# Four neighbouring tokens to a partition in a three-layer macaron kernel

## The reference, cut to what matters

```python
def _apply_rope(x, sin, cos):
    x1 = x[..., ::2]
    x2 = x[..., 1::2]
    r = jnp.stack([x1 * cos - x2 * sin, x1 * sin + x2 * cos], axis=-1)
    return r.reshape(x.shape)

q = (src @ Wq)...; k = (src @ Wk_c @ Wk)...; v = (src @ Wv_c @ Wv)...
sin, cos = _rope_sincos(Tt, DH)
q = _apply_rope(q, sin, cos)
k = _apply_rope(k, sin, cos)
attn = softmax(einsum('bhqd,bhkd->bhqk', q, k) / sqrt(DH))
x = _rmsnorm(src + (attn @ v) @ Wo, norm1_w)
# then an MLP and eight gated experts on x, token by token, and a second norm
```

## Time and profile before

| | |
|---|---|
| median of the runs | 834.25 us |
| the profiled execution | 834.06 us, of which its span is 832.0 us |
| TensorE busy | 804.7 us (97%) |
| VectorE busy | 664.6 us (80%) |
| ScalarE busy | 501.9 us (60%) |
| GpSimd busy | 353.5 us (42%) |
| mean granted TensorE clock | 0.997 |
| moved by DMA | 37.83 MB in 24700 packets |

### The profile page before, as it was taken

One profiled execution on the slowest core, in us unless ns is written; L12 is line 12 of the kernel. 1 busy time (PEld: TensorE's weight loads), 2 busy tenths in 40 slices (PEclk: granted clock), 3 DMA queues, 4 the chain that ended last, 5 costly groups with the idle time before them and its releaser, 6 DMA issues. The chain is left out here.

```text
span 832.0 us, 13459 instructions
## 1 busy us (share of the span) xinstructions
PE 804.7 (97%) x4436; PEld 308.7 (37%) x4438; DVE 664.6 (80%) x1303; ACT 501.9 (60%) x1073; POOL 353.5 (42%) x760
## 2 busy tenths in 40 slices
PE   8899999999999999999999999999999999999996
PEld 3323334334333343332323232233433434355453
DVE  6999987697789758887989999988988687673355
ACT  3267664475467627765877777777764475376441
POOL 2564328615331353424442357334253623442534
PEclk9999999999999999999999999999999999999999
DMA  4565203010200010020010323204102200000000
GB/s 119 129 168 128 81 2 78 19 58 11 70 2 2 20 62 2 9 74 3 3 51 32 78 81 83 76 14 107 37 21 58 77 2 14 1 15 2 1 13 14
DMA packets 24700, 37.83 MB, mean 45 GB/s; under 512 B 6464, under 2 KB 22080, under 8 KB 23048
## 3 DMA queue, kind: packets, MB, share of 16 engines
q1 hardware_dynamic: 24149, 36.25, 15.5%
q10 hardware_dynamic: 483, 0.74, 0.3%
HBM read 27.03 MB, written 9.11 MB: 43 GB/s over the span
## 5 line engine op out<-in xcount | busy, mean ns | idle before, releaser
L1387 ACT ACTIVATE probs<-ps 128x512 f32<-128x512 f32 x768 | 414.4, 598 | 228.0 <-PE ps L957 205.1
L1178 DVE TENSOR_REDUCE maxes<-ps 128x1 f32<-128x512 f32 x768 | 479.1, 681 | 47.6 <-PE ps L924 45.5
L924 PE MATMUL ps<-k_aug,q_aug 72*128 72x512 bf16 (+1 forms) x768 | 246.2, 382 | 3.5 <-ACT k_aug L1358 0.7
L957 PE MATMUL ps<-q_aug,k_aug 75*128 75x512 bf16 (+1 forms) x704 | 231.8, 383 | 3.3 <-DMA q_aug<-maxT 1.3
L984 PE MATMUL ps_out<-probs,v_aug 128*18 128x512 f32 x1408 | 185.4, 598 | 1.7 <-ACT probs L1387 1.0
L924 PEld LDWEIGHTS ps<-k_aug,q_aug 72*128 72x128 bf16 (+1 forms) x768 | 64.3, 96 | 162.8 <-issue 107.1
L1058 PE MATMUL ps<-w,hidden 128*128 128x512 f32 x256 | 118.7, 596 | 0.0
L957 PEld LDWEIGHTS ps<-q_aug,k_aug 75*128 75x128 bf16 (+1 forms) x704 | 59.0, 97 | 136.3 <-issue 88.9
L1279 DVE TENSOR_TENSOR prod<-ps,gate 128x512 f32<-128x512 f32 x56 | 38.7, 691 | 54.5 <-PE ps L1058 43.6
L1579 POOL TENSOR_TENSOR prod<-prod 128x512 f32<-128x512 f32 x28 | 35.5, 1268 | 85.2 <-DVE prod L1279 68.8
L1499 POOL TENSOR_SCALAR max_parts<-maxes 128x16 bf16<-128x16 f32 (+1 forms) x38 | 10.9, 288 | 141.6 <-DVE maxes L1178 141.4
(11 more groups left out here) (157 smaller groups left out, 755.3 us busy)
## 6 DMA issues: line engine op xcount, KB each, us to landing
q_aug<-qk_parts SPq DMA_DIRECT2D x7, 1152.0 KB
k_aug<-qk_parts SPq DMA_DIRECT2D x21, 384.0 KB
qk_parts<-parts SPq DMA_DIRECT2D x48, 128.0 KB, 2.3
q_aug<-qk_parts SPq DMA_DIRECT2D x11, 288.0 KB
k_aug<-qk_parts SPq DMA_DIRECT2D x27, 96.0 KB
qk_parts<-parts SPq DMA_DIRECT2D x24, 64.0 KB, 2.0
X<-in_x_dram SPq DMA_DIRECT2D x4, 256.0 KB, 4.6
w<-in_ffn_W_experts_dram SPq DMA_DIRECT2D x2, 512.0 KB, 5.8
```

Source lines behind the costliest of these rows:

```text
L924: pe.matmul(bank(use[i]), q_aug[p0:p1, r, at, qt * 128:(qt + 1) * 128], k_aug[p0:p1, r, at, :], start=True, stop=True).then_inc(bank_full[ ...
L957: pe.matmul(bank(use[i]), k_aug[p0:p1, r, at, kt * 128:(kt + 1) * 128], q_aug[p0:p1, r, at, :], start=True, stop=True).then_inc(bank_full[ ...
L1178: dve.tensor_reduce(maxes[:, u % 2, qt, at:at + 1], full(use[0]), AX.X, ALU.max).then_inc(bank_free[use[0][0]], 1)
L1387: act.activation(probs[:, step % P_RING, c:c + exp_run(u), :], both(use), ACT.Exp, scale=scale)\
```

## The change

A partition now holds four neighbouring tokens: token 4p + t lies in tile t of partition p. A load or store of a whole sequence moves 2048 contiguous bytes a partition where it moved four pieces of 512 bytes. The store of a single tile takes every fourth row of the output. Along the row of `xT`, column 128t + p is now token 4p + t, so every use of the tables reads them in that order: four runs of 128 elements, and within a run every fourth element (16 bytes apart). The other operand and the result are seen with the same shape, and are read and written contiguously. The tables themselves are loaded as before.

```diff
+        def by_tiles(a):
+
+            return a.rearrange("d (t p) -> d t p", p=128)
+
+        def table(a):
+            return a[:, :].rearrange("d (p t) -> d t p", p=128)
+
         def rotate(eng, seq, own_wait, u, qk):
 
             c, s, q = rotated(u, qk)
-            seq(eng.tensor_tensor(s, s, sinT[:, :], ALU.mult))
+            seq(eng.tensor_tensor(by_tiles(s), by_tiles(s), table(sinT), ALU.mult))
...
-            sp.dma_start(X[:, 0, :, :], x[0].rearrange("(t p) c -> p t c", p=128)).then_inc(x0_loaded, 16)
+            sp.dma_start(X[:, 0, :, :], x[0].rearrange("(p t) c -> p t c", p=128)).then_inc(x0_loaded, 16)
...
-                sp.dma_start(X[:, b, :, :], x[b].rearrange("(t p) c -> p t c", p=128)).then_inc(x_loaded, 16)
+                sp.dma_start(X[:, b, :, :], x[b].rearrange("(p t) c -> p t c", p=128)).then_inc(x_loaded, 16)
...
-                    sp.dma_start(out[b].rearrange("(t p) c -> p t c", p=128), X[:, b, :, :]).then_inc(stored, 16)
+                    sp.dma_start(out[b].rearrange("(p t) c -> p t c", p=128), X[:, b, :, :]).then_inc(stored, 16)
...
-                    sp.dma_start(out[batch(u), t * 128:(t + 1) * 128, :], X[:, batch(u), t, :]).then_inc(stored, 16)
+                    sp.dma_start(out[batch(u)].rearrange("(p t) c -> p t c", p=128)[:, t, :], X[:, batch(u), t, :]).then_inc(stored, 16)
...
-                    ins = dve.tensor_tensor(c, o, cosT[:, :], ALU.mult)
+                    ins = dve.tensor_tensor(by_tiles(c), by_tiles(o), table(cosT), ALU.mult)
...
-                        dve.tensor_tensor(s, full(use[1]), sinT[:, :], ALU.mult).then_inc(bank_free[use[1][0]], 1)
+                        dve.tensor_tensor(by_tiles(s), by_tiles(full(use[1])), table(sinT), ALU.mult).then_inc(bank_free[use[1][0]], 1)
```

## The result

| | before | after |
|---|---|---|
| median of 19 runs each | 835.39 us | 837.46 us |
| lowest run | 833.78 us | 837.03 us |
| profiled execution, span | 834.06, 832.0 us | 837.46, 835.5 us |
| TensorE, VectorE, POOL busy | 804.7, 664.6, 353.5 us | 807.0, 671.8, 358.4 us |

The ratio after to before is 1.0027, with a 95% interval of 1.0015 to 1.0039: slower beyond its interval, and within the 0.5% that the prediction calls "same". The traces and the lowest runs lie 3.3 to 3.5 us apart, the medians only 2.1 us. The kernel before came out at 835.39 us in these 19 runs, 1.1 us above the three runs on which the forecast stood.

The account below looks back on a forecast made before the run. VectorE bounds 21 to 48 us, both engines are nearly full 48 to 128 and 384 to 576, TensorE bounds 576 to 800. Terms -0.1 + 0 + 0.56 + 0.3 + 0.6 + 0.3 = +1.7 on 834.06 give 835.7 us, range 833.0 to 839.2.

Parts of the forecast that it names:

- x: What a stepped table read adds to one VectorE multiplication: taken as 0.2 us, range 0 to 0.52.
- Load, -0.1 us: First load of X, at the start: larger pieces save 0.1 us, bounds 0 and -1.0 us.
- Stores, 0: Only the last tile's store is on the path: no change, bounds -0.2 and +0.3 us.
- Start, 4x - 0.24: Unit 0: four stepped multiplications on VectorE's gapless chain, less 0.24 us of idleness, delay the start by 0.56 us.
- 21 to 48 us, 2x - 0.1: Two stepped multiplications where VectorE is the bound, less 0.1 us for small slack: 0.3 us.
- Later, a third of nine products: Of twelve later VectorE multiplications, a third of the nine where both engines are nearly full arrives: 3x = 0.6 us.
- POOL, +0.3 us: POOL's 14 sine-table multiplications: +0.46 us each, mostly covered, +0.3 us arriving for all.
- rival C: POOL's longer rotations delay the splits of maxima and stores queued behind them: +3.2 us, 837.9 us; chance 0.09.
- more than five waits for the split: TensorE's matmuls waiting for POOL's split of the maxima (L1507) more than five times would show the late-rotations rival.
- Rival B: VectorE needs a second cycle for each stepped element, 0.52 us a product: +4.5 us, 838.6 us; chance 0.22.
- A: The step is free on VectorE (x = 0): 834.1 us; chance 0.27.
- D: Pieces of 2048 bytes bring the first load forward by up to 1 us, x being small: 833.2 us; chance 0.08.

Follow-up runs that it names:

- e1: Changed kernel with both tables' columns laid out in DRAM in the order of use, so reads are contiguous: 833.75 us median, ratio to the kernel before 0.9968.
- e6: Kernel before with another kind of step in each unit (wrong angles): VectorE's product 0.68 us with the table by 8 bytes, 1.07 us by 32 bytes.
- e3: Kernel before with stepped table reads on VectorE alone (wrong angles): 838.12 us median, ratio 1.0025.
- e2: Kernel before with stepped table reads on both VectorE and POOL (wrong angles): 839.16 us median, ratio 1.0035.
- e10: The changed kernel repeated unchanged: 837.98 us median, ratio to the kernel before 1.0040.
- e8: e1 with sequences 1 to 3 loaded in pieces of 512 bytes as before (wrong angles for those): 834.10 us median.
- e4: Kernel before with stepped table reads on POOL alone (wrong angles): 837.05 us median, ratio 1.0014.
- e5: Kernel before with tables stepped only in units 3, 10 and 11 and for q of units 8 and 9 (wrong angles there): span 834.0 us in one run.
- e7: e1 with the first sequence loaded in pieces of 512 bytes as before (wrong angles for it): 835.57 us median, ratio to the kernel before 1.0016.
- e12: e1 repeated unchanged: 834.80 us median, ratio to the kernel before 0.9995.
- e9: e1 repeated unchanged on another chip: 834.60 us median, ratio to the kernel before 1.0000.
- e11: Changed kernel with two neighbouring tokens to a partition, pieces of 1024 bytes, tables read by 8 bytes: 835.82 us median, ratio to the kernel before 1.0005.

## Why the prediction was right

The sign, the bound within 0.5%, and the mechanism were right. The forecast of 835.7 us was 1.8 us under the measured 837.46, and the largest term that was off is the price x. As a difference the forecast was +1.7 us, beside +2.1 between the medians and +3.4 between the traces. That it lies so near the medians' is luck: the medians hold different shares of runs at a low clock, and the cost of the stepped reads that the traces show is twice the sum. Step by step:

- **Load, -0.1 us.** The norm starts 0.32 us earlier, in the mean of the profiles too. At the first product the means are 0.02 us apart, and profiles of like loads differ by up to 0.67. In e1, by 743 us, 0.07 us are left. So the runs show no gain of 0.1 us, and don't exclude one.
- **Stores, 0.** The last unit's stores land in 1.5 us as before.
- **x = 0.2 us.** This is the term of the sum that was mis-sized: 0.41 us. I argued that only one of three streams is stepped; e6 shows that one is enough, and that a second one (PSUM) adds nothing. The row that I read as the lower bound, runs of eight elements with gaps, does not bear on single elements: its runs are longer than 16 bytes, and they lie in PSUM, where e6 shows even a step of 16 bytes to be free on VectorE. The reciprocal's row also read PSUM, so it wasn't evidence either.
- **Start, 4x - 0.24.** With x = 0.40 that is 1.36 us, less the 0.13 us by which the first product began earlier: the cast was late by 1.22 us. But TensorE was late by 0.87 only, because 0.35 us of fillers lay between the cast and the matmul. "Within a few tenths" had been in the text as a remark and not in the sum.
- **21 to 48 us, 2x - 0.1.** 0.77 us measured, 0.7 by the formula.
- **Later, a third of nine products.** e3 has 2.53 - 1.20 = 1.33 us after 44 us, 3.2x: the sum of 3x was right. Its spread was not, so that it came out right is in part luck. k's products of units 8 and 9 gave 0.44 and 0.46 us, their whole extra, q's of these units and those of units 3, 10 and 11 next to nothing, and the stretch of unit 2 0.31 us, which is within the spread of profiles without a step. "A third of each" is a mean over places that pass all or nothing. Which ones pass could be read before the change: from 450 to 576 us TensorE waited for the swap at two places only, 0.18 and 0.23 us long, and these are the two.
- **POOL, +0.3 us.** The price was overrated (0.46 against 0.27 us each) and what arrives of it underrated (0.45 us in the changed kernel's profile, 0.9 to 1.0 in e2 and e10). I had looked for TensorE's five waits and found POOL idle before those splits. The delay arises at the other splits, those that follow a rotation without a gap. My own sign for rival C, more than five waits for the split, is no good: the changed kernel has six, but so has e3, where POOL's products are contiguous. The "half more" of the Trainium skill's "GPSIMD Engine Reference" (Performance pitfalls for Q7 kernels) is not reached by this instruction: a stepped table makes the whole product 21% longer. A step of 8 bytes is free, as the rule says.

Rival B had the right direction for x and too high an end (0.52). Its sum with x = 0.41 is +3.5 us, near the trace's +3.4. A (free) is refuted by the group means, and D (up to 1 us from the load) by the norm's start and by e1. Of C the price (+0.46 us) and the size (+3.2 us) are refuted, but its path, the split behind a rotation, is real.

## What to carry to other kernels

A view that looks free in the code can be paid for by element: before an operand in SBUF is read or written in steps, see whether two neighbours lie in the same 16 bytes. If they don't, lay the table out in the order of use when it is made. What a longer instruction costs is decided by who waits for it: look in the trace before the change for the places where the bounding engine already waits for this instruction or for what it frees. Here the extra of VectorE's products passed whole at such places and hardly at all elsewhere. And before a tenth of a microsecond is given to an edit, see how far profiles of the same kind lie apart: here their first products lay 0.67 us apart.

## What the runs showed of the hardware

- VectorE's product of 512 fp32 elements: 0.68 to 0.69 us with a step of 8 bytes or with pairs every 32 bytes, 1.05 to 1.19 us (group mean 1.09) with single elements every 16, 32 or 128 bytes, read or written in SBUF alike. A step of 16 bytes in the PSUM operand was free.
- On POOL one stepped stream, or an operand and result stepped in place, gave 1.51 to 1.59 us, and all three 2.12 us, against 1.27.
- In six of the 14 profiles (before, after, e1, e3, e8, e10) the granted clock fell to half for 3 to 4 us from about 35 us, where VectorE is the bound, and the lag shows no step there. In four others (e4, e5, e7, e12) it kept up there and fell to half from about 53 us, for 3.5 to 14 us, behind a wait for a load of maxima, and the lag rose there by 1.5 to 6.4 us. The last four (e2, e6, e9, e11) had neither. No profile had both. e12 had one more fall, at 336 us, and its lag rose by 1.6 us between 188 and 442 us. What decides between them was not found.
